# Four key tiles of the cross-attention moved into the end of the state scan, four value tiles into the second norm

## What is computed

```python
h = mamba_block(x, ...)                       # 16 states, scanned along the 512 positions
def attention_block(x, ...):                  # of the same layer
    xn = rmsnorm(x, norm_attn_w)              # "first norm" of the kernel (number 0)
    q, k, v = ...                             # 4 heads, 2 key/value heads
    attn = softmax(where(causal, -inf, q @ k.T * scale))
    x = x + (attn @ v) @ o_w.T
    xn = rmsnorm(x, norm_ffn_w)               # "second norm" (number 1)
    return x + silu(xn @ gate_w.T) * (xn @ up_w.T) @ down_w.T
...
# cross-attention, later in the layer, on the context alone:
kv = ctx @ Wkv.T
rk, rv = kv[..., :1024], kv[..., 1024:]       # keys: 1024 x 512 a batch, values: 512 x 1024 a batch
```

## Time and profile before

| | |
|---|---|
| runs without a profile | 2804.55, 2807.13 and 2814.09 us, median 2807.13 |
| profiled execution: its own time | 2809.64 us |
| profiled execution: span | 2807.8 us |
| busy share of the span | PE 91%, DVE 51%, ACT 39%, POOL 25% |
| mean granted clock of PE | 0.944 |

### The profile page before, as it was taken

One profiled execution on the slowest core, in us unless ns is written; L12 is line 12 of the kernel. 1 busy time (PEld: TensorE's weight loads), 2 busy tenths in 40 slices (PEclk: granted clock), 3 DMA queues, 4 the chain that ended last, 5 costly groups with the idle time before them and its releaser, 6 DMA issues. The chain is left out here.

```text
span 2807.8 us, 40095 instructions
## 1 busy us (share of the span) xinstructions
PE 2547.3 (91%) x16440; PEld 1558.8 (56%) x16441; DVE 1428.5 (51%) x2083; ACT 1091.4 (39%) x1885; POOL 709.6 (25%) x388
## 2 busy tenths in 40 slices
PE   7769999999999999999949978999999998599998
PEld 4346533754365534754338845364553644488887
DVE  5557437942876357832811124554455554644442
ACT  3674335822664255532512213444344433011111
POOL 0147027810865046901820020000000000022222
PEclk8979999999999999999979987999999998699999
DMA  5551002200030003100059930010010102044453
GB/s 199 212 190 34 0 1 86 78 1 1 1 140 24 1 0 123 41 1 1 1 190 331 340 126 18 1 24 23 19 28 1 24 8 98 12 160 159 159 178 91
DMA packets 62127, 219.26 MB, mean 78 GB/s; under 512 B 12293, under 2 KB 28122, under 8 KB 45178
## 3 DMA queue, kind: packets, MB, share of 16 engines
q1 hardware_dynamic: 45802, 187.39, 18.6%
q0 software_dynamic: 9568, 18.75, 2.7%
q10 hardware_dynamic: 6576, 10.57, 1.0%
HBM read 172.50 MB, written 39.99 MB: 76 GB/s over the span
## 5 line engine op out<-in xcount | busy, mean ns | idle before, releaser
L652 PE MATMUL psum<-arena 128*128 128x256 f32 (+7 forms) x4224 | 1085.1, 408 | 68.0 <-ACT arena L1528 11.5
L652 PEld LDWEIGHTS psum<-arena 128*128 128x128 f32 (+1 forms) x4224 | 672.9, 195 | 427.4 <-issue 313.1
L2495 POOL TENSOR_TENSOR arena<-arena 128x1024 f32<-128x1024 f32 x128 | 299.5, 2367 | 95.5 <-DVE arena L1996 80.9
L1996 DVE TENSOR_TENSOR_SCAN arena<-arena,psum 128x512 f32<-128x512 f32 x256 | 290.9, 1201 | 22.4 <-PE psum L793 14.5
L793 PEld LDWEIGHTS psum<-arena 128*128 128x128 f32 x2048 | 236.6, 193 | 49.3 <-ACT arena L1558 40.3
L793 PE MATMUL psum<-arena 128*128 128x128 f32 x2048 | 249.0, 279 | 2.0 <-issue 1.9
L2535 POOL DMA_INDIRECT arena<-xn,arena x32 | 31.6, 988 | 800.8 <-DVE arena L2437 793.5
L2502 POOL TENSOR_TENSOR arena<-arena 128x1024 f32<-128x1024 f32 x32 | 76.0, 2374 | 558.6 <-ACT arena L1649 558.6
L2097 DVE SCALAR_TENSOR_TENSOR arena<-psum,arena 128x1024 f32<-128x1024 f32 x128 | 156.0, 1245 | 90.5 <-PE psum L943 90.1
L1649 ACT ACTIVATE arena<-arena 128x1024 f32<-128x1024 f32 x128 | 147.1, 1149 | 44.2 <-DVE arena L2097 42.9
L1828 ACT ACTIVATE arena<-psum 128x256 f32<-128x256 f32 x128 | 49.1, 383 | 296.3 <-PE psum L652 294.9
(11 more groups left out here) (293 smaller groups left out, 3021.9 us busy)
## 6 DMA issues: line engine op xcount, KB each, us to landing
arena<-in_W SPq DMA_DIRECT2D x46, 1024.0 KB
arena<-c_rows SPq DMA_DIRECT2D x32, 512.0 KB, 4.0
arena<-in_Wg SPq DMA_DIRECT2D x16, 1024.0 KB, 4.8
arena<-in_Wu SPq DMA_DIRECT2D x16, 1024.0 KB, 7.5
arena<-in_Wd SPq DMA_DIRECT2D x16, 1024.0 KB, 10.0
arena<-in_xT SPq DMA_DIRECT2D x8, 512.0 KB, 6.1
zs_all<-arena SPq DMA_DIRECT2D x4, 1024.0 KB, 3.9
ut_all<-arena SPq DMA_DIRECT2D x4, 1024.0 KB, 8.8
```

What stands on the lines that cost most here:

```text
L652: r = mm(dst, w, x, start=i == 0, stop=i == len(pairs) - 1)
L1996: V.tensor_tensor_scan(hs[n % 3][:, c, :], dA[n % 2][:, c, :], bank[4 + c], 0.0, ALU.mult, ALU.add)\
L2495: nc.gpsimd.tensor_tensor(h, h, c_all[:, n % CBUFS, :].unsqueeze(1).broadcast_to([P, 2, L]), ALU.mult)\
```

## The change

Key tiles 4 to 7 leave the second norm and are computed at the end of the scan, in banks 4 to 7, each as soon as the last scan of its bank is done: tile 4 ahead of the sum of state 14, tiles 5 and 6 ahead of the sum of state 15, tile 7 behind it, ahead of the output projection. ACT empties them after its last work for the scan and signals `late_kept`; PE waits for that ahead of the first norm's sums, which use bank 5. The waits for the weights and the context move ahead of tile 4. Value tiles 1 to 4 leave the attention loop and take the places of keys 4 to 7 in the second norm; ACT empties two of them between its squares and its root and two behind the root. Value tile 0 stays in turn 0. The two lanes are numbered anew.

```diff
+                def late_key_tile(m):
+
+                    w(scan_done, KI * (NS - 1) + m - 3)
+                    acc(bank[m], [(w_xk[:, k, m * P:(m + 1) * P], ctxT[:, k, :]) for k in range(KD)])\
+                        .then_inc(late_keys.sem, 1)
...
+                    if n == NS - 2:
+                        pe.wait_ge(ld_w0.sem, 16 * len(w0_loads))
+                        pe.wait_ge(ld_ctx.sem, ld_ctx.at(32, b))
+                        late_key_tile(4)
+                    elif n == NS - 1:
+                        late_key_tile(5)
+                        late_key_tile(6)
                     w(hc_ready, 4 * (n + 1))
                     add_to_y(lambda i, j: ident[32 * i:32 * i + 32, 32 * i:32 * i + 32], hs[n % 3], stop=n == NS - 1)\
                         .then_inc(y_acc.sem, 1)
+                late_key_tile(7)
                 w(yz_ready, 2)
...
-                pe.wait_ge(ld_w0.sem, 16 * len(w0_loads))
-                pe.wait_ge(ld_ctx.sem, ld_ctx.at(32, b))
                 keys_tile(0)
                 keys_tile(1)
+                w(late_kept, 4)
                 norm_var(0)
...
-                    if i < 5:
-                        values_tile(i)
+                    if i == 0:
+                        values_tile(0)
                 weigh_v(U0 // 2 - 1)
...
-                keys_tile(4)
-                keys_tile(5)
+                values_tile(1)
+                values_tile(2)
                 norm_var(1)
-                keys_tile(6)
+                values_tile(3)
                 norm_rows(1)
-                keys_tile(7)
+                values_tile(4)
                 w(na.out, 2)
...
+                for m in range(4, 8):
+                    w(late_keys, m - 3)
+                    A_(xkT[:, m, :], bank[m], ACT.Identity).then_inc(late_kept.sem, 1)
                 w(LV.drained, LV.upto("out", 2))
...
-                    if 1 <= i < 6:
-                        drain_values(i - 1)
+                    if i == 1:
+                        drain_values(0)
...
-                norm_roots(1, hb)
+                norm_squares(hb)
+                drain_values(1)
+                drain_values(2)
+                norm_root(1, False)
+                drain_values(3)
+                drain_values(4)
...
-                norm_among_keys(1, 4, V_NF)
+                norm_out(1, xn, hb, V_NF)
```

More of the change, by code:

```diff
@@ L20 @@
 LH, LE, BLK = 16, 16, 64
-OT0_AT, XK = (3, 6, 7, 8), ("xk_a", "xk_b")
-XV_AT = [("att", i) for i in (0, 1, 2, 4, 5)] + [("xv", i) for i in range(3)]
+OT0_AT = (1, 2, 3, 4)
+XV_AT = [("att", 0)] + [("xvn", i) for i in range(4)] + [("xv", i) for i in range(3)]
 SBUFS, TBUFS, RBUFS = 3, 4, 2
@@ L392, in decoder_program @@
         yz_ready = sig("yz_ready", KI)
+        late_keys, late_kept = sig("late_keys", 4), sig("late_kept", 4)
         U0, HP = NC * 4, XH // 2
@@ L404, in decoder_program @@
         LA = Lane(sig("act_tile"), sig("act_drained"), bank[0:2],
-                  (("q", 2), ("k", 1), ("v", 1), ("att", 9), ("gate", KF),
+                  (("q", 2), ("k", 1), ("v", 1), ("att", 5), ("xvn", 4), ("gate", KF),
                    ("xv", 3), ("xq", 8), ("xn", 2)))
         LV = Lane(sig("dve_tile"), sig("dve_drained"), bank[2:4],
-                  (("out", 2), ("xk_a", 4), ("o", 2), ("xk_b", 4), ("up", KF - 1),
+                  (("out", 2), ("xk", 4), ("o", 2), ("up", KF - 1),
                    ("down", 2), ("xo", 2), ("logit", 1)))
@@ L765, in keys_tile @@
                 def keys_tile(m):
-                    project(LV, XK[m // 4], m % 4, w_xk, ctxT, m)
+                    project(LV, "xk", m, w_xk, ctxT)
+                def late_key_tile(m):
+                    w(scan_done, KI * (NS - 1) + m - 3)
+                    acc(bank[m], [(w_xk[:, k, m * P:(m + 1) * P], ctxT[:, k, :]) for k in range(KD)])\
+                        .then_inc(late_keys.sem, 1)
                 def values_tile(i):
@@ L895, in _ @@
                         transpose_o((i - 3) // 2)
-                    if i < 5:
-                        values_tile(i)
+                    if i == 0:
+                        values_tile(0)
                 weigh_v(U0 // 2 - 1)
                 transpose_o(NC - 1)
-                act_has("att", 9)
+                act_has("att", 5)
                 for m in range(2):
                     project(LV, "o", m, w_o, oT)
-                keys_tile(4)
-                keys_tile(5)
+                values_tile(1)
+                values_tile(2)
                 norm_var(1)
-                keys_tile(6)
+                values_tile(3)
                 norm_rows(1)
-                keys_tile(7)
+                values_tile(4)
                 w(na.out, 2)
@@ L1975, in take_keys @@
                 def take_keys(m):
-                    t = LV.take(dve, b, XK[m // 4], m % 4)
+                    t = LV.take(dve, b, "xk", m)
                     V.tensor_copy(xkT[:, m, :], t).then_inc(LV.drained.sem, 1)
[L1979 to L1986, removed]
                 def add_tile(group, m, dst, src):
@@ L2014, in _ @@
                     add_tile("out", m, hb[:, m, :], xln[:, m, :])
-                norm_among_keys(0, 0, V_NA)
+                take_keys(0)
+                take_keys(1)
+                norm_factor(0)
+                take_keys(2)
+                norm_apply(0, xn, hb, V_NA)
+                take_keys(3)
                 dve.wait_ge(ld_ctx.sem, ld_ctx.at(32, b))
```

## The result

| | median | runs |
|---|---|---|
| before | 2806.98 us | 2802.01 to 2814.09, 6 runs |
| changed | 2789.94 us | 2784.73 to 2796.89, 6 runs |
| ratio | 0.9938 | 95% interval 0.9924 to 0.9953 |

A second set of five runs gave 2789.03 against 2807.65, 18.6 us, ratio 0.9933 (0.9919 to 0.9946). The profiled execution of the first set has a span of 2785.0 us.

The account below looks back on a forecast made before the run. PE, busy 91% of the span, was examined stretch by stretch; the scores, maxima, exponentials chain was taken to set the loop's turns. 18.0 + 1.6 = 19.6 us, from 2809.64 to 2790.0, forecast 2788 against the median, range 2778 to 2800.

Parts of the forecast that it names:

- The attention loop: Turns 1 to 4 without value tiles: the scores, maxima, exponentials chain sets the pace; 4.49 us won a batch, 18.0 in all.
- the four hand-overs to ACT: Attention loop: scores of turns 2 to 5 start 0.05 us behind ACT's read; gains 0.81, 1.03, 1.30 and 1.35 us.
- The end of the scan: Four key tiles fill PE's 3.98 us idle a batch, the clock stays up, the projection shortens; 1.6 us won over the batches.
- The second norm: Value tiles replace key tiles, PE's list keeps its length, ACT's emptying is hidden; uncovered it would cost 7.5 us in all.
- the root's delay: Second norm: ACT's root comes 0.2 us later, hidden behind a tile on PE with 0.9 us to spare.
- The clock in the thinned loop: Rival: idle pieces of 0.4 to 0.9 us in four turns drop the clock; lasting half clock gives 2834 us; chance 0.07.
- the late last sum: End of the scan: the last sum starts 2.9 us later than before, as two tiles stand ahead of it.
- the bound of the whole loop: Rival in the attention loop: all 16 tiles come off PE's time, 29 us won in all, 2778; chance of below 2782: 0.07.
- The second warning of the Trainium skill: Attention loop: small idle pieces between matmul groups cycling through PSUM banks make the clock swing; given a small chance.

Follow-up runs that it names:

- the loop alone: Against the kernel before: value tiles 1 to 4 move to the second norm, key tiles 4 to 7 stay there too; 2822.32 us against 2805.95, ratio 1.0057.
- The filler: Kernel before plus three matmuls nothing reads, two ahead of the scan's last sum and one ahead of the output projection; 2796.92 us, ratio 0.9966.
- the swapped order: Changed kernel with ACT taking the second norm's root before it empties value tiles 1 and 2; one run, 2805.28 us.
- the version made from it: Changed kernel with value tile 0 ahead of turn 1's scores, value tile 1 halved over turns 1 and 2, key tile 6 in the second norm; 2782.18 us, 0.9908.
- tile 6 moved: Changed kernel with key tile 6 moved from ahead of the scan's last sum to behind it; ratio 0.995 to the kernel before.
- the filler in the second norm: Late keys at the scan's end, value tiles left in the loop, three unread matmuls in the second norm's waits; ratio 0.9998 to the kernel before.

## Why the prediction came out right

*The attention loop* was right in mechanism and size: 4.49 us a batch predicted, 4.48 or 4.49 in each, and the four hand-overs to ACT stand in the rows. The run with the loop alone shows the same 10.85 us without the late keys in three batches of four.

*The end of the scan* was right in mechanism and a little too good in size: the sum had 1.6 us won, the traces show 0.84. Tile by tile the list came out (projection predicted 10.50 us behind the sum of state 13, measured 10.60; the end predicted at 17.46, measured 17.55). What was mis-sized is batches 2 and 3, where I took the loss to be 0.2 us from the projection's length alone; there the projection also began earlier than in batch 1 (8.21 and 7.99 us behind the sum of state 13, batch 1 8.35), so they too lose 0.46. In each batch the list also came out 0.1 us longer than summed. That the clock would hold is what carried this step. The filler shows it directly: with no other change, filled gaps give back 11 us in the trace. By it, the tiles aren't free: against filled gaps the four batches take 10.2 us more, so without what the clock gives back the step would have been a loss of some 10 us.

*The second norm*: the root's delay was hidden, as predicted, and the swapped order shows that PE is held as soon as a tile's bank comes late.

*The clock in the thinned loop*, my rival on the slower side, did not come: from turn 2 to turn 6 the time is 10.85 or 10.86 in every batch. It falls elsewhere. At the start of the loop, where PE waits 0.69 and 1.41 us, it fell in one batch of the profile before and one after, and over all profiles in none to four of the four batches. There the prediction had such a fall at 1.2 us at most; it costs 1.63 (6.33 - 4.70) in batch 0 before. In the second norm the clock fell where tiles were missing or late, and in one batch each of the changed kernel's second profile and of the version made from it without that (1.7 us). Nor did the late last sum cost anything (tile 6 moved, no gain), and PE was not the bound of the whole loop.

The sum was 19.6; the two rows of the table that the change moves give 18.8, and the medians of two sets 17.0 and 18.6. One loss is in no term of the sum: the third norm of batch 0, from its sums of squares to the scores of the cross-attention, takes 22.39 us instead of 20.69, at a clock of 0.75 and 0.83 in two windows of 4 us at its start. It does so in both profiles of the changed kernel and in the run with tile 6 moved, and not in the profile before; with it the traces give 17.1 us. Why the clock falls just there is not shown. The 22.8 us between the two spans hold more that is not the change: from the cross-attention's output projection of batch 3 to the end, where the program is the same, the profile after takes 1412.1 us and that of before 1419.0, and the sum of state 13 of batch 0 starts 1.35 us later after than before, behind a program that is the same too.

The second warning of the Trainium skill that I had weighed ("TensorE: Matmul & The Clock Gate", "A second HAM failure mode: psum-queue depth-cycling", that small idle pieces between groups of matmuls make the clock swing) didn't hold for the thinned turns, whose idle pieces are 0.35 to 0.90 us at a clock of 1.00; the second norm of the swapped order is nearer to it, where a wait of 0.84 us was followed by a tile at a clock of 0.57.

## What to carry to other kernels

Where two chains share PE, look in each turn for who is late: a tile that PE does last in a turn costs only the time between the moment its successor could start and the moment PE is free, here 0.8 to 1.35 us of 1.74. Work moved into a wait of PE also decides the clock of what follows: three matmuls of filler a batch were worth 9 us here, and norm steps stripped of their tiles gave back on the clock what they won in length. Count PE's gaps by stretch, and move tiles from stretches where PE is full to turns where it waits, in halves if a whole one doesn't fit.

## What the runs showed of the hardware

Behind a wait of 0.84 us that followed the sums of squares, the next 128x512 tile took 3.5 to 3.7 instead of 1.9 us in four batches of four (clock 0.57 in batch 1), while turns with waits of 0.90, 0.67, 0.35 and 0.36 us one after the other kept the clock at 1.00. With the filler in the second norm, waits of 0.24 and 0.56 us around the sums of squares came with a clock of 0.69. So the length of PE's waits doesn't tell alone whether the clock falls. What PE did before may count (matmuls of one column in the norm, scores and transposes in the turns); no run here separates the two.

The same program text, from the last cross-attention projection to the end, took from 1412.1 to 1422.0 us in the profiles of this case, so single executions differ by 10 us where nothing was changed. A gain of 17 us is read from traces stretch by stretch, or from medians of several runs, not from two spans.
